# The scan of a Mamba block with MLP: statistics of x1 moved to the middle of the tile, the sum of residual and h moved to GpSimd

## The reference, cut to what matters

```python
def block1(x):
    xn = rmsnorm(x)                        # mamba2: projection, causal conv of 4 taps, silu,
    h = x + mamba2(xn, ...)                # chunked state scan with 8 heads of 64, gate with silu(z),
                                           # rmsnorm, w_out
    m = square(relu(rmsnorm(h) @ w_fc)) @ w_proj
    return h + m
x1 = layernorm(x + block1(x))              # = layernorm((x + h) + m)
h = silu(x1 @ w1) * (x1 @ w2)              # then two layers of 1024x1024 with gelu, and w3
out = layernorm(x1 + ffn(x1))
```

## Time and profile before

| | |
|---|---|
| median of 3 runs | 1225.28 us (1225.24 to 1225.66) |
| the profiled execution: its time, its span | 1226.21 us, 1224.5 us |
| TensorE matmul, weight load | 98%, 82% of the span |
| VectorE, ScalarE, GpSimd | 64%, 52%, 19% of the span |

### The profile page before, as it was taken

How to read it: one execution, slowest core, us unless ns; L and a number is a source line. 1 busy time by engine, 2 the same in 40 slices (tenths; PEclk the granted TensorE clock), 3 DMA queues, 4 the chain that set the end, 5 groups by cost and what they waited for, 6 DMA issues and landing times.

```text
span 1224.5 us, 19168 instructions
## 1 busy us (share of the span) xinstructions
PE 1195.6 (98%) x6412; PEld 1003.1 (82%) x6412; DVE 783.8 (64%) x1370; ACT 639.2 (52%) x1199; POOL 237.7 (19%) x210
## 2 busy tenths in 40 slices
PE   8899999999999999999999999999999999999996
PEld 7677888888887888788888888888888888888885
DVE  6798898989999898855535337345363363543633
ACT  6687888878788878666224124142141331422420
POOL 0517253443435261720000000000000000000000
PEclk9999999999999999999999999999999999999998
DMA  8214131333324141334500202002002020020000
GB/s 294 71 65 126 65 81 72 105 99 101 105 78 128 58 124 64 99 128 172 211 1 1 52 1 51 0 0 51 0 6 45 0 51 0 0 51 0 18 1 19
DMA packets 92169, 79.40 MB, mean 65 GB/s; under 512 B 63200, under 2 KB 81760, under 8 KB 90208
## 3 DMA queue, kind: packets, MB, share of 16 engines
q1 hardware_dynamic: 92128, 78.86, 20.8%
HBM read 66.77 MB, written 25.70 MB: 76 GB/s over the span
## 4 chain that ended last, share of the span: by engine, by line
issue 53%; POOL 0%; DVE 0%; POOLq 0%; DVEq 0%
POOL rsv_b L1937 0%; DVE o_sb L2014 0%; POOLq L1935 0%; DVEq L1768 0%; POOL rsv L237 0%; POOLq L450 0%
## 5 line engine op out<-in xcount | busy, mean ns | idle before, releaser
L1921 ACT ACTIVATE full<-bank,scale 128x512 f32<-128x512 f32 x128 | 88.3, 690 | 383.0 <-PE bank L1830 383.0
L1830 PE MATMUL bank<-hB_hi,h_sb 128*128 128x512 f32 x512 | 199.6, 390 | 0.0
L1830 PE MATMUL bank<-hB_lo,h_sb 128*128 128x512 f32 x512 | 199.6, 390 | 0.0
L1830 PE MATMUL bank<-hA_hi,h_sb 128*128 128x512 f32 x512 | 199.3, 389 | 0.0
L1830 PE MATMUL bank<-hA_lo,h_sb 128*128 128x512 f32 x512 | 199.3, 389 | 0.0
L1983 DVE CAST hA_hi<-full 128x512 fp32r<-128x512 f32 x64 | 27.3, 427 | 173.1 <-ACT full L1921 173.1
L1937 POOL TENSOR_TENSOR rsv_b<-mv_b,eps 128x4 f32<-128x4 f32 x8 | 10.7, 1340 | 618.2 <-DVE mv_b L189 618.2
L1830 PEld LDWEIGHTS bank<-hA_hi,h_sb 128*128 128x128 f32 x512 | 96.1, 188 | 20.1
L1830 PEld LDWEIGHTS bank<-hA_lo,h_sb 128*128 128x128 f32 x512 | 96.1, 188 | 20.1
L1830 PEld LDWEIGHTS bank<-hB_hi,h_sb 128*128 128x128 f32 x512 | 96.3, 188 | 19.2
L1830 PEld LDWEIGHTS bank<-hB_lo,h_sb 128*128 128x128 f32 x512 | 96.2, 188 | 19.0
(11 more groups left out here) (231 smaller groups left out, 2967.6 us busy)
## 6 DMA issues: line engine op xcount, KB each, us to landing
chk_xh<-w_ffn SPq DMA_DIRECT2D x16, 704.0 KB, 4.2
ffn_raw<-w_ffn SPq DMA_DIRECT2D x8, 1408.0 KB, 7.0
h_sb<-ffn_raw SPq DMA_DIRECT2D x2, 4096.0 KB, 19.0
xT<-x_t SPq DMA_DIRECT2D x8, 512.0 KB, 3.9
x_res<-x SPq DMA_DIRECT2D x8, 512.0 KB, 3.8
x_rows<-x SPq DMA_DIRECT2D x8, 512.0 KB, 3.5
x_in<-x_rows SPq DMA_DIRECT2D x8, 512.0 KB, 4.7
x_in<-x SPq DMA_DIRECT2D x7, 512.0 KB, 4.7
```

The lines of the kernel that those rows point to most:

```text
L1830: ins = pe.matmul(o, a_, b_, start=first and n == 0, stop=last and n == 1, skip_group_check=True)
L1921: nc.scalar.activation(full[:, n % FULL, :], b[:], ACT.Gelu, scale=scale[:, 1 + n // KH, n % KH:n % KH + 1]).then_inc(s_gd, 1)
```

## The change

Of VectorE's list of tile i, `norm_x1(i - 2)` goes from the first place to the place behind `add_out(1)`, as `stats_x1` and `norm_x1_tail`, which do the same operations. `x_plus_h(i - 1)` goes from VectorE's list, where it stood between `scores(0)` and `y_diag(0)`, to GpSimd's, behind `make_ud(1)` and in front of `decay_state(1)`. `x1_rstd(i - 2)` on GpSimd goes from behind `decay_state(1)` to behind the `m_lo_part` of 6, in front of `make_ud(3)` and `decay_state(3)`. The last tile's `x_plus_h` and the norm of tile 6, outside the lists, stay on VectorE as they are.

```diff
@@ -225,6 +225,19 @@
                 nc.vector.scalar_tensor_tensor(
                     out=x1[:, c, :], in0=pj_banks[c // 2][:, (c % 2) * D:(c % 2 + 1) * D],
                     scalar=r2h[:, c:c + 1], in1=xh[:, c, :], op0=ALU.mult, op1=ALU.add).then_inc(s_pjd, 1)
+
+        def stats_x1(dve, t):
+
+            step = Steps(dve, s_ls, STAT_STEPS * t)
+            dve.wait_ge(s_pjd, CH * t + CH + 1)
+            for c in range(CH):
+                step.mark(nc.vector.bn_stats(bn[:, c, :], x1[:, c, :]))
+            return step
+
+        def norm_x1_tail(step):
+            step.wait(step.n)
+            layer_norm_tail(step, bn, mv, EPS_LN).then_inc(s_mv, 1)
+            assert step.n == STAT_STEPS
 
         def norm_x1(dve, t):
             step = Steps(dve, s_ls, STAT_STEPS * t)
@@ -1279,6 +1292,11 @@
                     nc.gpsimd.tensor_tensor(heads(y[:, c % 2, :]), heads(xt[:, c % 2, :]), bc(dskip_b[:]),
                                             ALU.mult).then_inc(s_skip, 1)
 
+                def x_plus_h(t, w):
+                    pool.wait_ge(s_pjd, CH * t + 1)
+                    pool.wait_ge(s_dd, w.dve(f"wo{CH - 1}") + 1 + DVE_BANKS)
+                    nc.gpsimd.tensor_tensor(xh, x_res[:], h[:], ALU.add).then_inc(s_xh, 1)
+
                 def decay_state(i, c):
                     b, o = c % 2, 1 - c % 2
                     pool.wait_ge(s_sup, CH * i + c + 1)
@@ -1287,7 +1305,8 @@
                     nc.gpsimd.tensor_tensor(heads(S[:, o, :]), heads(S[:, b, :]),
                                             bc(dec[:, 2, c * HEADS:(c + 1) * HEADS]), ALU.mult).then_inc(s_sdec, 1)
 
-                def iteration(w, i, mlp, more, norm):
+                def iteration(w, i, before, more, norm):
+                    mlp = before is not None
                     make_skip(w, i, 0)
                     make_u(w, i, 0)
                     chunk_totals(i)
@@ -1301,9 +1320,9 @@
                     make_u(w, i, 1)
                     make_skip(w, i, 1)
                     make_ud(w, i, 1)
+                    if mlp:
+                        x_plus_h(i - 1, before)
                     decay_state(i, 1)
-                    if norm:
-                        x1_rstd(pool, i - 2)
                     make_u(w, i, 2)
                     make_u(w, i, 3)
                     make_ud(w, i, 2)
@@ -1314,6 +1333,8 @@
                     make_skip(w, i, 3)
                     if mlp:
                         m_lo_part(i - 1, 6)
+                    if norm:
+                        x1_rstd(pool, i - 2)
                     if more:
                         make_ud(w, i, 3)
                         decay_state(i, 3)
@@ -1321,11 +1342,11 @@
                     if more:
                         decay_operands(w, i + 1)
 
-                iteration(w_first, 0, False, True, False)
-                iteration(w_loop(1), 1, True, True, False)
+                iteration(w_first, 0, None, True, False)
+                iteration(w_loop(1), 1, w_first, True, False)
                 with pool.Fori(2, TILES - 1) as i:
-                    iteration(w_loop(i), i, True, True, True)
-                iteration(w_last, TILES - 1, True, False, True)
+                    iteration(w_loop(i), i, w_loop(i - 1), True, True)
+                iteration(w_last, TILES - 1, w_loop(TILES - 2), False, True)
                 x1_rstd(pool, TILES - 2)
 
             @block.vector
@@ -1529,8 +1550,6 @@
                     mlp = before is not None
                     per = F_STEPS + CM_STEPS
                     step = Steps(dve, s_ds, HEAD_STEPS + per * i - (1 if mlp else 0))
-                    if norm:
-                        norm_x1(dve, i - 2)
                     mask_exponents(w, 0)
                     if mlp and not norm:
                         turn_squares(i)
@@ -1538,8 +1557,6 @@
                     if mlp:
                         y_off(w, i, 0)
                     scores(w, i, 0)
-                    if mlp:
-                        x_plus_h(i - 1, before)
                     y_diag(step, w, i, 0)
                     mask_exponents(w, 2)
                     state(step, i, 0)
@@ -1587,6 +1604,10 @@
                     if more:
                         tap(step, w, i + 1, 4, 1)
                     add_out(w, i, 1)
+                    if norm:
+                        x1_step = stats_x1(dve, i - 2)
+                    if norm:
+                        norm_x1_tail(x1_step)
                     yT(w, 2)
                     y_diag(step, w, i, 3)
                     if more:
```

## The result

The changed kernel takes 1229.51 us in the median (1229.11 to 1231.24, 5 runs), the kernel before 1225.24 us beside it (1224.04 to 1225.66, 5 runs): the ratio is 1.0039, 95% interval 1.0025 to 1.0052. Slower, by about 4.3 us; the forecast was 1230.8, and slower by more than 0.2% had the largest chance, 0.69.

The account below looks back on a forecast made before the run. TensorE's matmul list was taken to bound the kernel, following VectorE's chain, lengthened by GpSimd, before out_rows(0). Tiles 2 to 6 at 0.3 + 0.7 us each, plus the last tile and tile 1, added 5.5 us: 1230.8, range 1225.0 to 1233.5.

Parts of the forecast that it names:

- Statistics leave the front, gain 0: Before y_diag(0): VectorE gets 4.3 us free, TensorE gains nothing, since scores(0) still waits for GpSimd's decay.
- x_plus_h, 2.35 us: Estimated duration of x_plus_h on GpSimd, where no profile row showed two full 1024-wide operands being added.
- First term, +0.3 by the loss of the spacer: Before out_rows(0): without the rstd between gate and u(2), u(2) delays scores(1); +0.3 us a tile.
- the gap in front of yT_lo's exponents: Sign in TensorE's weight loads: idle time before yT_lo's exponent matmul would grow from 0.59 to 0.9 us.
- Second term, +0.7: Second place, behind out_rows(0): rstd delays ud(3) and last decay into tmp and tap of chunk 3; +0.7 us a tile.
- The move itself costs nothing: Behind add_out(1): the statistics, 2.25 us, are covered by VectorE's 1.98 us wait for yT_hi(2).
- The last tile: It has the first delay, before out_rows(0), but no ud(3): 0.3 to 0.6 us lost.
- Tile 1: It already lacked the rstd between gate and u(2): 0 to 0.2 us lost.
- R1: Only one term acts: the second alone 1228.8 us, the first alone 1227.1; chance 0.25 (0.14 and 0.11).
- R2: Hidden: the chain regains its loss from earlier u(1) and short x_plus_h, no second term; 1224.4 to 1225.5 us, chance 0.10.
- R3: Faster: scores(1) before u(2), x_plus_h through before m_lo, TensorE's waits vanish, 0.8 us a tile; 1220.8 us, chance 0.08.
- R4: Worse: x_plus_h at 2.5 us or m_lo in the tail, 2 us a tile; 1235 us, chance 0.07.

Follow-up runs that it names:

- a_xph_back: Changed kernel with x_plus_h back in its old place on VectorE: 1231.21 us, ratio 1.0028 to 1.0062.
- a_spacer: Changed kernel with a four-element power on GpSimd at the rstd's old place: 1227.59 us, ratio 1.0 to 1.0023.
- b_rstd: Kernel before with only the rstd moved, to in front of ud(3): 1227.07 us, ratio 1.001 to 1.0033.
- a_rstd_late: Changed kernel with the rstd behind the last decay instead of in front of ud(3): 1229.51 us, ratio 1.0028 to 1.0053.
- a_early: Changed kernel with ud(3) and the last decay moved up behind GpSimd's m_lo of 4: 1227.10 us, ratio 1.0002 to 1.002.
- a_both: Changed kernel with the four-element power at the rstd's old place and ud(3) with the last decay earlier: 1223.98 us, ratio 0.998 to 0.9999.
- v_spacer: Changed kernel with x_plus_h first on VectorE, rstd behind the last decay, four-element power at the rstd's old place: 1229.24 us.
- v_hold: Changed kernel with x_plus_h first on VectorE, rstd behind the last decay, u(2) held until norm_x is done: 1230.12 us.
- w_all: Changed kernel with x_plus_h first on VectorE, ud(3) and last decay earlier, u(2) held for norm_x, u(3) for xn_lo: 1224.11 us.

## Why the prediction was right, and where it was not

*What bounds the kernel* held: every difference between the kernels' tiles lies in the stretches in which TensorE stands for VectorE. The one exception is the lower clock in tile 6 of a_xph_back.

*Statistics leave the front, gain 0*: right for the front, 11.16 against 11.19 us. Behind it the credit was too small: ud of chunk 1 ends 3.10 us behind the load of `y_diag(0)` instead of 3.97, so 0.87 earlier, not 0.72, and the gate 0.44 us ahead, not 0.3.

*x_plus_h, 2.35 us*: it took 376.38 - 374.10 + 0.10 = 2.38.

*First term, +0.3 by the loss of the spacer*: the mechanism is shown by a_spacer, the size was 0.15. It is a difference of two larger numbers, which the table gives: +0.60 for the rstd's leaving (b_rstd), -0.45 for x_plus_h's leaving VectorE when the statistics have left too (a_xph_back to changed). An error of 0.15 us in the earlier u(1) halved the result. One sign that I had named was wrong: the gap in front of yT_lo's exponents did not grow from 0.59 to 0.9 but fell to 0.34, since TensorE now stands 0.46 us one step earlier, in front of y_diag(1), for `scores(1)`.

*Second term, +0.7*: 0.66. The order of events in the changed kernel was that predicted: tap 1.53 us, gate 1.07 late where 1.2 was said, add_out(3) 0.8 where 1.0 was said. But the step "The move itself costs nothing", with the price laid to the rstd in front of ud(3), assigned the cause wrongly, and that the size came out at 0.66 does not bear it out. a_rstd_late undid that order and got nothing back. b_rstd made that order without the statistics and lost nothing there; this alone would also fit my account, in which the rstd waits for the statistics. The price belongs to the statistics in the middle: they take the 1.98 us from ud(3) and the decay, which then meet either the tail (a_rstd_late) or tmp and the tap (changed). My sentence called that pause a cover for VectorE's work; it was GpSimd's as well. Nor is it the length of the statistics: in a_early they stand in the same place, only ud(3) and the decay are out of their way, and the second place is that of before.

*The last tile*, 0.3 to 0.6: 0.33. *Tile 1*, 0 to 0.2: `scores(1)` took 2.06 us there before and takes it after; in the executions at full clock the first `sum_x1` starts within 1 us of each other (155.9 to 156.9 us), whichever kernel it is, which leaves room for a few tenths and shows none.

*The sum*: 0.8 a tile for 1.0 forecast and 0.33 for about 0.5 in the last tile, which is most of the 1.3 us between 1230.8 and 1229.5.

*The rivals.* R1 needs one term at zero: the first is at half its size, so the time came close to "the second alone" (1228.8) without being that. R2's claim that the chain regains what it loses is three quarters true (-0.45 against +0.60), and fails by the second term. R3's condition, `scores(1)` in front of u(2), was made true in a_both: it gives 0.40 us a tile, not 0.8, since `out_rows(0)` still waits 0.93 us for tmp. Its second condition, x_plus_h through before m_lo, holds in v_spacer, v_hold and w_all, where x_plus_h is back on VectorE, and brings no more: from y_diag(1) on the chain hangs on TensorE itself. R4's m_lo in the tail did not occur.

## What to carry to other kernels

When a step leaves a place between two engines that share a port, ask what kept its neighbours apart: here a four-element power was worth 0.5 us a tile by standing in front of a large operation. A pause of one engine is not free room if the other works in it: look at both timelines before filling it. And cost a collision in both orders before blaming the order, since undoing the order alone may only move the wait.

## What the runs showed of the hardware

Small operations pay like large ones. In a_rstd_late a 128x4 `TENSOR_TENSOR` took 1.04 us instead of 0.16, and a `TENSOR_SCALAR` with one input 0.90 instead of 0.17, each until the GpSimd operation beside it ended. The four `bn_stats` did not wait: 1.40 us for the four under GpSimd's m_lo. The Trainium skill (SBUF — State Buffer, "Who interferes with whom") says that `tensor_scalar`, if its operands meet certain conditions, can enter a mode in which it takes the ports shared with GpSimd as well; the 0.90 us agrees.

Who is first goes by hundredths of a us: two operations that start 0.01 to 0.03 us apart swap from tile to tile (b_rstd, v_spacer), at 0.6 to 0.7 us each time. The start shown does not decide it at this resolution: GpSimd starts 0.01 us ahead in tile 4 of both kernels, and goes first in b_rstd and second in v_spacer.

The granted clock of the first 40 us differs between executions of one program. The profiled one of before had 0.83 from 10 to 20 us, with 0.63 us for a 128x512 matmul, that of the changed kernel 1.00 there, with 0.39; the first `sum_x1` started at 158.84 in the one and 156.72 in the other. The matmuls of 0.63 us, from 16.66 to 19.2, are the level of 1.2 GHz, those of 0.39 that of 2.4, and 0.83 is the mean over the stretch; in both executions TensorE had run 128x8 and 128x16 matmuls up to 15.2 and 15.6 us and then stood 0.3 to 0.5 us for VectorE. Four other profiled executions at 1.00 up to 40 us had their first `sum_x1` at 155.9 to 156.9, eight with a lower clock somewhere in it at 158.0 to 159.1. So these 2.1 us go with the clock, and not with which kernel it is; with 0.8 more behind the seventh of the eight `sum_x1`, where the table ends, they are why the profiled spans differ by 3.1 us and the tiles by 4.4, and why tile lengths tell apart what medians hardly do.
